# Moving the cross-attention zero point from VectorE to ScalarE, with the stage around it reordered

## The reference

```python
def fake_quant(x, scale, zp):
    q = jnp.clip(jnp.round(x / s + z), 0.0, 255.0)
    return (q - z) * s
x = x + attention(layernorm(x), Wq, Wk, Wv, Wo)
x = x + fake_quant(layernorm(x), x1_scale, x1_zp) @ fake_quant(ctx_4096, x2_scale, x2_zp)
x = x + linear_q8_8(layernorm(x), ffn_weight, ffn_bias)   # integers: x and weights times 256
```

## Time and profile before

| | |
|---|---|
| median of 3 runs (lowest, highest) | 468.59 us (468.58, 468.93) |
| the profiled execution: its own time | 469.95 us |
| its span, first to last instruction | 468.1 us |
| TensorE matmuls busy | 434.2 us, 93% |
| VectorE busy | 381.5 us, 81% |
| ScalarE busy | 293.3 us, 63% |
| GpSimd busy | 287.6 us, 61% |
| mean granted TensorE clock | 0.989 |

### The profile page before, as it was taken

One profiled execution on the slowest core, in us unless ns is written; L12 is line 12 of the kernel. 1 busy time (PEld: TensorE's weight loads), 2 busy tenths in 40 slices (PEclk: granted clock), 3 DMA queues, 4 the chain that ended last, 5 costly groups with the idle time before them and its releaser, 6 DMA issues.

```text
span 468.1 us, 9435 instructions
## 1 busy us (share of the span) xinstructions
PE 434.2 (93%) x3602; PEld 234.3 (50%) x3602; DVE 381.5 (81%) x961; ACT 293.3 (63%) x294; POOL 287.6 (61%) x157
## 2 busy tenths in 40 slices
PE   0899999998999999999999999999999978599796
PEld 0776455544555555555555555555544433255342
DVE  5899875888888898988988998994366799889585
ACT  3686251334779777778879889888631527346643
POOL 6002463245899999999988898889610868703000
PEclk9999999999999999999999999999999999599999
DMA  8473454922340111110153321334294512015155
GB/s 334 173 281 113 147 192 154 303 73 81 94 123 25 48 58 47 58 58 27 46 181 114 115 84 41 105 115 137 90 314 181 113 47 55 13 25 111 36 188 209
DMA packets 37937, 55.11 MB, mean 118 GB/s; under 512 B 21632, under 2 KB 27008, under 8 KB 36608
## 3 DMA queue, kind: packets, MB, share of 16 engines
q1 hardware_dynamic: 36592, 45.99, 31.4%
q10 hardware_dynamic: 1296, 8.45, 5.2%
HBM read 40.67 MB, written 9.44 MB: 107 GB/s over the span
## 4 chain that ended last, share of the span: by engine, by line
PE 61%; POOL 20%; DVE 7%; DMA 4%; ACT 3%; issue 3%; SPq 1%; POOLq 0%; ACTq 0%; DVEq 0%
PE ps L1489 15%; PE ps L1309 14%; POOL more L1226 6%; PE ps L1619 5%; PE ps L1391 5%; PE ps L1334 5%; POOL s1reg L1226 4%; POOL wkv L1226 4%; PE ps L1356 4%; PE ps L1375 4%; PE ps L1586 3%; POOL s1reg L1218 2%; POOL s1reg L1222 2%; DMA qstack<-in_x 2%; PE ps L1377 2%
## 5 line engine op out<-in xcount | busy, mean ns | idle before, releaser
L849 DVE CUSTOM_DVE_ANT_0 ps<-ps,causal 128x512 f32<-128x512 f32 (+3 forms) x256 | 121.0, 511 | 12.4 <-PE ps L1356 9.4
L601 ACT ACTIVATE s1reg<-ps 128x1280 f32<-128x1280 f32 x64 | 78.9, 1233 | 36.7 <-PE ps L1377 36.6
L1309 PE MATMUL ps<-xT,wqx 128*128 128x512 f16 x384 | 94.8, 379 | 0.0
L1489 PE MATMUL ps<-wo_reg,xT 128*128 128x512 f16 x384 | 92.5, 379 | 0.0
L1356 PE MATMUL ps<-kreg,qstack 96*128 96x512 f16 (+3 forms) x256 | 60.5, 300 | 1.9 <-DVE mt L849 1.9
L1375 PE MATMUL ps<-qstack,kreg 98*128 98x512 f16 (+3 forms) x256 | 57.2, 300 | 0.9 <-ACT s1reg L601 0.9
L1489 PEld LDWEIGHTS ps<-wo_reg,xT 128*128 128x128 f16 x384 | 36.7, 97 | 37.3 <-issue 0.2
L1309 PEld LDWEIGHTS ps<-xT,wqx 128*128 128x128 f16 x384 | 36.7, 97 | 36.2 <-issue 0.3
L1226 POOL TENSOR_TENSOR s1reg<-s1reg 128x1280 f16<-128x1280 f32 x19 | 49.7, 2625 | 4.6 <-ACT s1reg L607 4.5
L1207 POOL TENSOR_TENSOR s1reg<-s1reg 128x512 f32<-128x512 f32 x11 | 16.0, 1451 | 58.7 <-DVE s1reg L838 58.6
L1226 POOL TENSOR_TENSOR wkv<-s1reg,wkv 128x1280 f16<-128x1280 f32 x18 | 47.0, 2623 | 4.8 <-ACT wkv L607 4.8
(11 more groups left out here) (129 smaller groups left out, 909.1 us busy)
## 6 DMA issues: line engine op xcount, KB each, us to landing
s1reg<-in_weights ACTq DMA_DIRECT2D x8, 1024.0 KB, 5.6
s1reg<-in_ctx SPq DMA_DIRECT2D x16, 512.0 KB, 4.3
qstack<-rope_scratch SPq DMA_DIRECT2D x48, 128.0 KB, 2.6
rope_scratch<-s1reg SPq DMA_DIRECT2D x40, 128.0 KB, 2.2
qstack<-in_x SPq DMA_DIRECT2D x8, 512.0 KB, 5.6
s1reg<-in_x SPq DMA_DIRECT2D x16, 256.0 KB, 3.3
out<-s1reg SPq DMA_DIRECT2D x7, 512.0 KB, 3.6
s1reg<-in_L_ffn_weight SPq DMA_DIRECT2D x5, 512.0 KB, 6.7
```

Source lines behind the costliest of these rows:

```text
L601: nc.scalar.activation(ebuf[:, j % 2, :], st_ps[:, 0:SCORES], ACT.Exp, scale=EXP_SCALE, bias=P_LOG_SCALE).then_inc(e_done, 1)
L849: last = nc.vector.tensor_tensor_reduce(part, part, causal[:, T - w:T], 1.0, LOWEST, ALU.add, ALU.max, mt[:, G % 2, h, qt:qt + 1])
L1309: last = mm(out_ap, w(ws, k), xT[:, xs, KT * b + k, :], start=(k == 0 and n == 0), stop=(k == KT - 1 and n == 2))
L1489: last = mm(ps[:, bank, :], xT[:, os, KT * b + k, t], wo_sb[:, ws, 4 * h:4 * h + 4, k, :], start=(k == 0 and n == 0), stop=(k == KT - 1 an ...
```

## The change

ScalarE's new `q1_zero_point(t)` reads the bytes, adds minus the zero point (a new column of `qs`, made once in the setup) and sums the result in the same instruction; VectorE's subtraction and ScalarE's summing copy go, and so does the semaphore `q1_sum`. The calls of the stage stand in another order on all five engines. The diff, with lines that did not change left out:

```diff
@@ -143,7 +143,6 @@
...
-        junk = wkvf[:, 2048:2560].bitcast(F16)
...
@@ -204,7 +203,6 @@
...
-        q1_sum = sem("q1_sum")
...
@@ -454,18 +452,18 @@
...
+            residual(13)
             q1_transpose(0)
-            residual(13)
+            residual(14)
             q1_transpose(1)
             q1_transpose(2)
-            residual(14)
...
+            q1_transpose(7)
             xq_transpose(0)
-            q1_transpose(7)
...
@@ -667,11 +665,12 @@
...
-            def q1_total(t):
-                act.wait_ge(q1_done, t + 1)
-                if t:
-                    act.wait_ge(q1_sum, t)
-                nc.scalar.activation(junk, q1[:, t % 2, :], ACT.Copy, accum_out=ra[:, 0, t:t + 1]).then_inc(q1_sum, 1)
+            def q1_zero_point(t):
+                act.wait_ge(ln_affine, t + 1)
+                if t >= 2:
+                    act.wait_ge(q1t_in[t % 2], 16 * (t // 2))
+                nc.scalar.activation(q1[:, t % 2, :], bytes8[:, t % 2, :], ACT.Identity, bias=qs[:, 19:20],
+                                     accum_out=ra[:, 0, t:t + 1]).then_inc(q1_done, 1)
...
@@ -705,52 +704,52 @@
...
+            q1_zero_point(0)
             ln_q1(1)
-            q1_total(0)
+            q1_zero_point(1)
             ln_q1(2)
             ln_q1(3)
-            q1_total(1)
-            q1_total(2)
+            q1_zero_point(2)
             rstd(LN2 + 1)
+            rstd(LN2 + 2)
+            weight_int_high(0)
+            q1_zero_point(3)
             ln_q1(4)
-            q1_total(3)
-            rstd(LN2 + 2)
+            weight_int_high(1)
+            rstd(LN2 + 3)
             ln_q1(5)
-            q1_total(4)
-            ln_q1(6)
-            weight_int_high(0)
-            weight_int_high(1)
+            q1_zero_point(4)
             weight_int_high(2)
             weight_int_high(3)
-            q1_total(5)
+            q1_zero_point(5)
             weight_int_high(4)
+            ln_q1(6)
+            q1_zero_point(6)
             weight_int_high(5)
-            q1_total(6)
             weight_int_high(6)
-            rstd(LN2 + 3)
+            ln_q1(7)
+            q1_zero_point(7)
             rstd(LN3 + 0)
-            ln_q1(7)
...
-            q1_total(7)
...
+            ft_high(2)
+            ft_high(3)
             rstd(LN3 + 1)
-            ft_high(2)
             ln_xq(4)
-            ft_high(3)
+            ln_xq(5)
+            acc_shift(0)
+            rstd(LN3 + 2)
+            acc_shift(1)
             ft_high(4)
-            ln_xq(5)
-            rstd(LN3 + 2)
-            acc_shift(0)
-            acc_shift(1)
             ln_xq(6)
             ln_xq(7)
+            acc_shift(2)
             ft_high(5)
-            acc_shift(2)
...
@@ -782,6 +781,7 @@
...
+                link(nc.vector.tensor_scalar(qs[:, 19:20], qs[:, 6:7], -1.0, None, ALU.mult))
...
@@ -1012,14 +1012,6 @@
...
-            def q1_zero_point(t):
-                dve.wait_ge(ln_affine, t + 1)
-                if t >= 2:
-                    dve.wait_ge(q1t_in[t % 2], 16 * (t // 2))
-                    dve.wait_ge(q1_sum, t - 1)
-                nc.vector.tensor_scalar(q1[:, t % 2, :], bytes8[:, t % 2, :], qs[:, 6:7], None,
-                                        ALU.subtract).then_inc(q1_done, 1)
-
...
@@ -1097,86 +1089,78 @@
...
-            stats2(1)
-            columns(0)
-            stats2(2)
             ctx(14, 0)
             output_add(9)
+            ctx(15, 1)
+            stats2(1)
+            stats2(2)
             stats2(3)
+            variance(LN2 + 0)
+            stats2(4)
             output_add(10)
-            variance(LN2 + 0)
+            output_add(11)
             inverse(LN2 + 0, 1.0)
-            stats2(4)
-            ctx(15, 1)
-            q1_zero_point(0)
-            output_add(11)
-            q1_zero_point(1)
-            q1_zero_point(2)
             stats2(5)
-            columns(1)
+            columns(0)
             output_add(12)
             output_add(13)
-            q1_zero_point(3)
             variance(LN2 + 1)
+            inverse(LN2 + 1, 1.0)
             stats2(6)
-            inverse(LN2 + 1, 1.0)
-            context_add(0)
-            context_stats(0)
-            q1_zero_point(4)
+            variance(LN2 + 2)
+            columns(1)
+            inverse(LN2 + 2, 1.0)
             output_add(14)
-            variance(LN2 + 2)
-            inverse(LN2 + 2, 1.0)
-            context_add(1)
-            context_stats(1)
-            q1_zero_point(5)
-            q1_zero_point(6)
...
+            context_add(0)
+            variance(LN2 + 3)
+            context_stats(0)
+            inverse(LN2 + 3, 1.0)
+            context_add(1)
+            context_stats(1)
             weight_int_low(1)
+            weight_int_low(2)
             context_add(2)
-            weight_int_low(2)
+            weight_int_low(3)
             context_stats(2)
-            weight_int_low(3)
             weight_int_low(4)
-            variance(LN2 + 3)
...
-            inverse(LN2 + 3, 1.0)
             inverse(LN3 + 0, FRAC)
+            context_add(4)
             weight_int_low(5)
-            q1_zero_point(7)
-            context_add(4)
+            weight_int_low(6)
             context_stats(4)
             context_add(5)
-            weight_int_low(6)
+            bias_int()
+            weight_int_low(7)
+            context_add(6)
+            ft_low(0)
+            ft_low(1)
             context_stats(5)
-            ft_low(0)
-            weight_int_low(7)
+            ft_low(2)
+            context_add(7)
             variance(LN3 + 1)
-            ft_low(1)
-            context_add(6)
+            ft_low(3)
             inverse(LN3 + 1, FRAC)
-            context_add(7)
+            needs_low(0)
             context_stats(6)
-            ft_low(2)
-            ft_low(3)
+            set_flag(0)
             context_stats(7)
-            needs_low(0)
-            set_flag(0)
             variance(LN3 + 2)
+            inverse(LN3 + 2, FRAC)
             ft_low(4)
-            bias_int()
             layer_bias(0)
-            inverse(LN3 + 2, FRAC)
             layer_out(0)
+            layer_bias(1)
             ft_low(5)
-            layer_bias(1)
             layer_out(1)
-            layer_bias(2)
             ft_low(6)
             ft_low(7)
+            layer_bias(2)
...
@@ -1253,7 +1237,7 @@
...
-                pool.wait_ge(q1_sum, t + 1)
+                pool.wait_ge(q1_done, t + 1)
...
@@ -1272,17 +1256,17 @@
...
+            weight_int(2)
             corrections(1)
-            weight_int(2)
             weight_int(3)
-            corrections(2)
             weight_int(4)
             weight_int(5)
+            corrections(2)
+            weight_int(6)
             corrections(3)
             corrections(4)
-            weight_int(6)
+            corrections(5)
             weight_int(7)
-            corrections(5)
...
@@ -1659,41 +1643,41 @@
...
+            output_b1(13)
             column_sums(1)
-            output_b1(13)
+            output_b1(14)
+            output_b1(15)
             context(0)
-            output_b1(14)
             context(1)
-            output_b1(15)
+            gram_weight(0)
             context(2)
-            gram_weight(0)
+            gram_weight(1)
             context(3)
-            gram_weight(1)
...
+            context(6)
             gram_weight(5)
-            context(6)
...
+            high_products(0)
             gram_x(1)
-            high_products(0)
-            high_products(1)
             gram_x(2)
             gram_x(3)
+            high_products(1)
             sum_flags(0)
             low_products(0, low)
-            gram_x(4)
...
+            high_products(4)
+            gram_x(4)
             gram_x(5)
-            high_products(4)
...
```

## The result

The changed kernel took 461.93 us in the median of 4 runs (461.05 to 464.45), against 468.58 us (468.22 to 468.93): a ratio (its time over that of the kernel before) of 0.9862 with a 95% interval of 0.9839 to 0.9885, 6.65 us faster. The forecast was 459.9 us in a range of 457.2 to 465.6. The profiled execution took 461.05 us, and its span is 459.3 us; the forecast for these two was 461.2 and 459.4. So the schedule was foreseen almost to the place, and the median less well (2.0 us above); the experiments are about that difference too.

A forecast was written before the change was run, and what follows sets the result against it. It took TensorE, with about 16 us of holes and half clock in the last 124 us, to set the end; the second flag's product 8.7 us sooner and an unchanged tail gave 459.9 us, range 457.2 to 465.6.

The forecast's parts named there:

- Step 1, the zero point: Zero point moved from VectorE to ScalarE: VectorE loses 10.5 us, each new activation takes 1.14 us, ScalarE's surplus is hidden.
- Step 2, outputs first: TensorE runs batch 1's outputs ahead of the context tiles: projections end at 383.8 us, with 0.35 us lost at add 10.
- Steps 3 and 4: ScalarE's queue and context tiles 0 to 3: nothing late, 3.32 us transfer wait gone, holes 1.5, 0.9, 1.2 us, end 402.5.
- Step 5: Context tiles 4 to 7 to the flags: coefficients at 409.6 us, low products 0 and 4 at 429.0 and 444.0.
- Step 6, the tail: The last 50 matmuls and epilogue stay the same, 15.4 us.
- the last line of the sum: 8.7 us off the profiled span, 468.1 to 459.4 us, and off the median, 468.59 to 459.9 us.
- The first (the clock falls in a hole): Holes at three context tiles make TensorE's clock fall once, price 2.9 + 0.4 us: 463.2 us; chance 0.15.
- The second (low weights held by GpSimd): Low weights ahead of context adds cost 2.66 us instead of 0.5, two such: 464.6 us; chance 0.12.
- The third rival: First context add after 390.4 us, clock halves, four context tiles at 6.53 us instead of 3.61: 474.0 us; chance 0.07.

The follow-up runs named there:

- r2: The changed kernel's new orders, but the zero point stays a subtraction on VectorE, at chosen places: 473.51 us, ratio 1.009 to the kernel before.
- r1: The kernel before with only the zero point moved to ScalarE, the other engines' orders old: 468.97 us, ratio 0.9993 to the kernel before.
- r4: The changed kernel again, no edit, eight runs on a second chip: median 465.68 us, ratio 0.9913 to the kernel before.
- r11: The changed kernel with the load of x piece 9 issued later, behind weight tile 5: 467.22 us, ratio 0.9958 to the kernel before.
- r6: The changed kernel without GpSimd's two long additions to x for tiles 3 to 7: 462.48 us, ratio 0.9847 to the kernel before.
- r0: The kernel before again, no edit, 12 runs: median 469.79 us, ratio 1.0016 to reference runs of the same kernel.
- r10: The two-bank-pair variant of the changed kernel (r8), with x pieces 9 to 11 loaded earlier: 462.75 us, ratio 0.9862 to the kernel before.
- r9: The changed kernel with x pieces 9 to 11 loaded earlier and the bias last: 462.93 us, ratio 0.9878 to the kernel before.
- r12: The kernel before with the load of x piece 9 issued later: 469.05 us, ratio 1.0002 to the kernel before.
- r3: The changed kernel with outputs 13 to 15 and contexts 0 to 2 in turns again: 482.89 us, ratio 1.028 to the kernel before.
- r8: The changed kernel with context tiles alternating two bank pairs, output add 10 and context add 4 moved ahead: 462.16 us, ratio 0.9854 to the kernel before.

## Why the prediction was right, and where it was off

- *What bounds the kernel.* Right: the gain is TensorE's holes and its low clock (0.50 and 0.54). The stage from output add 8 to the end takes 459.3 - 343.28 = 116.0 us instead of 468.1 - 343.75 = 124.35, 8.3 us less, where 8.7 was summed. Another 0.47 us of the profiled pair's difference lie ahead of the stage (343.28 against 343.75) and are luck; without them the places below would all be that much later, and the product of the second flag would stand at 444.3 for 444.0. That a tensor_scalar or tensor_tensor of VectorE waits until the GpSimd instruction beside it is over holds for L801 (1.10 us at 388.25 in the trace of before, ended at 389.35, GpSimd's L1261 at 389.34) and for L1020 (2.93 us at 365.85 beside L1261, 0.75 at 363.29 with no GpSimd instruction), but it is too wide: L794 took 0.14 us at 387.65, inside L1261 (386.67 to 389.34), and L1026 1.34 us at 370.38 beside GpSimd, as at 347.75 without it. That it is a port they wait for, as the prediction and the expectation of r2 word it, no run shows; the runs show the waits.
- *Step 1, the zero point.* 1.14 us was the value taken, halfway between two measured bounds, and 1.141 us is the mean of the eight. Hidden, as said. But VectorE's 10.5 us are worth nothing alone (r1), and without them the order is worth less than nothing (r2, at the places chosen for the subtractions). The prediction treated the first as a relief and credited the order with the sum; it had no term for their depending on each other.
- *Step 2, outputs first.* Right in size: the end at 383.6 for 383.8, the hole at output 12 of 0.49 for 0.35. One thing was missing: with the statistics moved behind it, VectorE waits at add 9 for a transfer, 4.1 us in the profile, and output 12 has no slack for it. The prediction bounded add 10's x and took for granted that "the x tiles come in time".
- *Steps 3 and 4.* Right: zero point 3 done at 385.8 (386.2 was said), the holes 1.47, 1.02 and 1.02 (1.5, 0.9, 1.2), the fourth tile's matmuls done at 402.3 (402.5). The transfer of 3.32 us that was to go was on the chain, but TensorE idled only 0.24 us for it, since tile 6 ran meanwhile; the sum did not use it. It was late not only because q1 of tile 7 was made late (ready at 417.7 us): SP issued it at 420.00, behind `xq_transpose(0)`, which the new list puts second.
- *Step 5.* Coefficients at 409.77 for 409.6, flags' products at 428.7 and 443.9 for 429.0 and 444.0.
- *Step 6, the tail.* 15.45 us for 15.4.
- *The weakest step* is the last line of the sum: it took the 8.7 us of one profiled pair off the median. The profiled execution of before lay 1.4 us above its median, that of after 0.9 below; the medians differ by 6.65 us in the first measurement, by 3.4 us in r4. That 6.65 us lie near the forecast is partly luck: a second measurement of the same kernel gave half. In r4 the changed kernel is also more uneven than the one before beside it. A likely reason is that it has a wait on a transfer and near meetings of VectorE and GpSimd ahead of an output and a context tile without slack, which r11 shows at one place; the clock behind the flag (r6) and the stage ahead of 344 us (r0) are rivals that no run tells apart, and the kernel before itself spread over 3.9 to 6.7 us on the other chips. The prediction's range (457.2 to 465.6) held the first median and not r4's, which lies 0.1 us outside.
- *The rivals.* The first (the clock falls in a hole) did not happen in the profiled execution: the holes between context tiles, 1.47, 1.02 and 1.02 us, left the clock at 1.00. It did happen in r11 after a hole of 2.58 us, in r10 after one of 2.20, and behind the flag in r6 after 1.28 and 0.86 (clocks of 0.73, 0.87 and 0.62 in the stretches behind them). One of the changed kernel's first four executions, 464.45 us, shows a mean clock of 0.989 where the other three show 0.998; it is 2.5 us above the median, and the rival's price was 3.3. With r4's lower mean clocks this says that the chance of 0.15 was too low. The second (low weights held by GpSimd) did not either: the pair at 395.21 took 2.13 us, 0.69 more than the 1.44 without GpSimd's instructions (r6); r11's took 4.33. Its price was also mis-summed: 2.66 instead of 0.5 us, twice, is 4.3 us and not 4.7. The third rival (a late first add, from there growing to a loss) is what r2 did, there for want of the lighter list: its first context add came at 391.02 us and the time was 4.5 us above before, by two holes over 3 us (4.48 and 3.63) and one slow tile (5.98), not by four slow tiles. The two tiles behind the slow one, each after a hole of 1.02 us, took 3.61 us at a clock of 1.00.

## What to carry to other kernels

When a load is taken off a busy engine and the time does not move, look whether the engine's waits grew elsewhere; here the part that freed VectorE and the part that used the freed time were worth 0 and -4.5 us alone and +6.65 together (+3.4 in r4). Before statistics or other filler is moved behind an add, read when that add's transfer lands: filler ahead of a wait is slack. Without it an add that began 3.9 us later cost 4.3 us (r11 against r9, medians), while the kernel before hid a delay of 1.9 us at that add (r12). A difference between two profiled executions is not the difference of the medians; ask for the spans of several.

## What was not expected of the hardware

- VectorE's small scalar_tensor_tensor on two columns waits for GpSimd too at times: L804 took 0.96 us at 375.88 us in the changed kernel's profile, beside GpSimd's L1254, and 0.16 at its other places there.
- The length of a hole did not settle whether the granted clock fell. It fell after holes of 2.58 us (r11) and 2.20 us (r10), and behind the flag after 1.28 and 0.86 us (r6) and after 1.16 and 0.86 us (r3, where 44 matmuls took 11.34 us at 0.85). It stayed at 1.00 after 2.41 us in the kernel before, after 2.19 us at r10's place (r8), and after 1.16 and 0.86 us behind the flag in the changed kernel.
- The same kernel's executions spread over 6.5 us in r4 (eight runs) and 3.4 us in the first measurement (four).
